# Two attention layers on one core: statistics, weight preparation and one subtraction of the second attention stage moved to other rounds

## The reference

```
x = x + attn_b(layernorm(x))      # q,k,v = x @ W + b; softmax(q k^T / 2) v; @ Wo + bo
x = x + ffn(layernorm(x))         # x @ (weight * scale).T + bias
```

## Time and profile before

| | |
|---|---|
| median of 3 runs | 1218.68 us (1216.99 to 1219.45) |
| profiled execution | 1217.67 us, span 1215.9 us |
| mean granted TensorE clock | 0.848 |
| PE busy | 998.3 us (82%) |
| PE weight loads | 879.1 us (72%) |
| DVE busy | 717.8 us (59%) |
| ACT busy | 367.5 us (30%) |
| POOL busy | 318.7 us (26%) |
| chain that ended last | PE 58%, DVE 22%, issue 6%, POOL 4% |

### The profile page before, as it was taken

The page is one execution under the profiler, slowest core; times in us unless marked ns, Lnnn a source line. Parts: engine busy times, 40 slices in busy tenths (PEclk is TensorE's granted clock), DMA queues, the critical chain, the costliest instruction groups (busy, mean ns, idle before and its releaser), DMA issues.

```text
span 1215.9 us, 21334 instructions
## 1 busy us (share of the span) xinstructions
PE 998.3 (82%) x8146; PEld 879.1 (72%) x8146; DVE 717.8 (59%) x1323; ACT 367.5 (30%) x663; POOL 318.7 (26%) x352
## 2 busy tenths in 40 slices
PE   3589987656378877777888999998888887799998
PEld 3466655446267766655657999998888887799998
DVE  4468876344476678888675545445566655644453
ACT  2136554403122212334334322321122221232232
POOL 4101221024853754212111022100333332230000
PEclk9679999877778888999769999986677775599999
DMA  8736340000020000455420000235666665210000
GB/s 232 218 110 178 115 133 2 2 0 10 26 71 18 1 1 18 141 164 174 130 71 1 2 1 1 62 79 105 131 130 118 144 120 97 35 36 10 18 18 18
DMA packets 147430, 89.38 MB, mean 74 GB/s; under 512 B 109633, under 2 KB 136257, under 8 KB 146561
## 3 DMA queue, kind: packets, MB, share of 16 engines
q1 hardware_dynamic: 142960, 70.45, 24.1%
q10 hardware_dynamic: 2944, 12.59, 3.6%
q0 software_dynamic: 1424, 4.98, 1.4%
HBM read 54.16 MB, written 33.55 MB: 72 GB/s over the span
## 4 chain that ended last, share of the span: by engine, by line
PE 58%; DVE 22%; issue 6%; POOL 4%; ACT 4%; SPq 3%; DMA 2%; DVEq 0%; ACTq 0%; POOLq 0%
PE SC L373 15%; PE SC L2144 9%; PE OT L373 8%; PE pb L373 7%; PE pa L373 5%; DVE mx L1318 3%; PE OT L1892 3%; PE SC L1845 2%; PE OT L2171 2%; PE SC L1874 2%; DVE OS L1486 2%; PE pa L2339 2%; DMA b_Q<-q_groups 1%; PE SC L2050 1%; DVE ON L1675 1%
## 5 line engine op out<-in xcount | busy, mean ns | idle before, releaser
L373 PE MATMUL SC<-xT_h,w_h 128*128 128x256 f32 x512 | 147.3, 288 | 10.3 <-DVE xT_l L1735 7.8
L373 PE MATMUL SC<-xT_l,w_h 128*128 128x256 f32 x512 | 145.8, 285 | 0.0
L373 PE MATMUL SC<-xT_h,w_l 128*128 128x256 f32 x512 | 145.0, 283 | 0.0
L373 PEld LDWEIGHTS SC<-xT_h,w_h 128*128 128x128 f32 x512 | 97.5, 190 | 13.9 <-DVE xT_l L1735 11.5
L373 PE MATMUL OT<-w,Qs 128*128 128x256 f32 x768 | 104.3, 285 | 2.2 <-DVE Qs L1745 1.4
L1318 DVE TENSOR_REDUCE mx<-SC 128x4 f32<-128x1024 f32 x64 | 78.1, 1221 | 43.5 <-PE SC L1845 43.1
L373 PEld LDWEIGHTS OT<-w,Qs 128*128 128x128 f32 x768 | 96.5, 191 | 2.9 <-DVE Qs L1745 1.6
L373 PEld LDWEIGHTS SC<-xT_h,w_l 128*128 128x128 f32 x512 | 97.9, 191 | 0.0
L373 PEld LDWEIGHTS SC<-xT_l,w_h 128*128 128x128 f32 x512 | 97.2, 190 | 0.0
L1741 DVE TENSOR_TENSOR hidden_f<-SC,silu_gate 128x512 f32<-128x512 f32 x64 | 44.1, 689 | 75.5 <-ACT silu_gate L1198 75.5
L2339 PE MATMUL pa<-ident,xn 128*128 128x128 f32 x192 | 35.8, 318 | 62.0 <-DVE xn L1451 27.1
(11 more groups left out here) (413 smaller groups left out, 2684.9 us busy)
## 6 DMA issues: line engine op xcount, KB each, us to landing
Qs<-q_stack SPq DMA_DIRECT2D x56, 128.0 KB, 3.1
k_stack<-KT_h SPq DMA_DIRECT2D x16, 256.0 KB, 2.4
k_stack<-KT_l SPq DMA_DIRECT2D x16, 256.0 KB, 3.0
q_stack<-QT_h SPq DMA_DIRECT2D x16, 256.0 KB, 2.6
q_stack<-QT_l SPq DMA_DIRECT2D x16, 256.0 KB, 3.3
b_Q<-q_groups SPq DMA_DIRECT2D x64, 64.0 KB
o_groups<-b_O ACTq DMA_DIRECT2D x8, 512.0 KB, 3.0
Qs<-q_stack SPq DMA_DIRECT2D x56, 64.0 KB, 3.2
```

The source lines that it names most:

```text
L373: ins = pe.matmul(out_ap, left[a], right[b], start=first and n == 0, stop=last and n == len(terms) - 1, **more)
```

## The change: what it does

Nothing is added or removed; instructions are moved among rounds.

- B0 `stats` goes from offset -17 to -21, `rstd_of` from -16 to -20. `normalise` stays at -14.
- GpSimd's jobs get other rounds. The four r1 weights come at -19, -11, -3 and 5 (before 1, 3, 5, 7), w1 at 13 (10), b1_q at 16 (22), w3 at 21 (16), b1_k 24 (24), b1_v 30 (26), b1_o 32 (28), w2 at 46 (40). The butterflies come at 29, 31, 37, 38, 39 and 45 (before 32 to 37), the mask products from 48 (46).
- VectorE's `x_low` of B0 comes ahead of `heads_out` in its round.
- F3's normalise, bias, transposes and low part come one round later.

```diff
--- before.py
+++ after.py
@@ -426,7 +426,7 @@
             return due(n, 31 + offset if s == F1 else offset)
 
         H_SLOTS = {F1: dict(stats=1, rstd=2, xn=3, bias=4, xT=5, low=6, y=7, res=7),
-                   F3: dict(stats=1, rstd=2, xn=3, bias=4, xT=4, low=5, y=7, res=8)}
+                   F3: dict(stats=1, rstd=2, xn=4, bias=5, xT=5, low=6, y=7, res=8)}
 
         def h_psum(s, b):
 
@@ -731,7 +731,8 @@
                     pool.sem_inc(stack_clear, 1)
 
             A0_JOBS = {8: "f0", 24: "b0_q", 32: "b0_k", 40: "b0_v", 48: "b0_o"}
-            B0_JOBS = {1: "r1_q", 3: "r1_k", 5: "r1_v", 7: "r1_o", 10: "w1", 16: "w3", 22: "b1_q", 24: "b1_k", 26: "b1_v", 28: "b1_o", 40: "w2"}
+            B0_JOBS = {-19: "r1_q", -11: "r1_k", -3: "r1_v", 5: "r1_o", 13: "w1", 16: "b1_q", 21: "w3", 24: "b1_k", 30: "b1_v", 32: "b1_o", 46: "w2"}
+            BUTTERFLIES = (29, 31, 37, 38, 39, 45)
 
             for K in K_rings["attn_a0"]:
                 for r in (32, 96):
@@ -820,16 +821,16 @@
                 if st.kind == "narrow":
                     return narrow_at
                 def wide_at(g):
-                    for b in due(g, -16):
+                    for b in due(g, -20):
                         rstd_of(b)
                     for b in due(g, -13):
                         row_bias(b)
                     if g in B0_JOBS:
                         prepare([B0_JOBS[g]])
-                    if 32 <= g < 38:
-                        butterfly(g - 32)
-                    if 46 <= g < 62:
-                        cut_mask(g - 46)
+                    if g in BUTTERFLIES:
+                        butterfly(BUTTERFLIES.index(g))
+                    if 48 <= g < 64:
+                        cut_mask(g - 48)
 
                 return tokens_at if st.kind == "tokens" else wide_at
 
@@ -1502,11 +1503,11 @@
                             maximum(b, t)
                     for b in due(g, 5):
                         max_low(b)
+                    for b in due(g, -12):
+                        x_low(b)
                     for c in range(CT):
                         for b in due(g, 10 + 2 * c):
                             heads_out(b, c)
-                    for b in due(g, -12):
-                        x_low(b)
                     for b in due(g, 13):
                         a_low(b)
                     for b in due(g, -10):
@@ -1517,7 +1518,7 @@
                         low(b, b0_Q, pb, "qh", bq, "ql")
                     for b in due(g, -5):
                         v_out(b)
-                    for b in due(g, -17):
+                    for b in due(g, -21):
                         stats(b)
                     for b in due(g, -14):
                         normalise(b)
```

## The result

The changed kernel takes 1202.9 us (median of 11 executions, 1200.4 to 1206.2) where the kernel before takes 1218.7 (11 executions): a ratio of 0.9877 with a 95% interval from 0.9848 to 0.9905. The gain is 15.8 us. I had forecast 26.1, and 1202.9 is above the upper end of my range. The profiled execution took 1206.06 us with a span of 1204.3 and a mean granted clock of 0.846. First the page of the changed kernel: busy times, and the granted clock in 40 slices of about 30 us.

A forecast was written before the change was run, and what follows sets the result against it. GpSimd's late root left a hole in B0; chain and residual adds set its beat. 18.9 - 1.4 + 4.4 + 5.35 - 0.3 - 0.9 = 26.1 off 1217.67 gives 1191.6, or 1192.6 as median; range 1181.5 to 1200.5.

The forecast's parts named there:

- steps 1 to 3: B0's fill, its hole at element 3, then its beats element by element; together 26.1 us gained.
- the fill: B0's first rounds up to 312.3 us: nothing changes; 0.3 to 1.0 us if VectorE's cover is gone.
- element 1: B0's beat of element 1: w3's subtraction delays F3's first normalise; 25.4 against 24.0, 1.4 us lost.
- elements 5 to 7: B0's last beats: F3's normalise stands ahead of work that others await; 0.3 and 0.9 us lost.
- Step 2, the hole: Normalise of element 3 runs at once at 312.3; first residual add at 326.6 instead of 345.47, 18.9 us gained.
- after 330: Sign of being wrong: B0's first residual add standing after 330 us, where 326.6 was forecast.
- Step 1: The fill: with GpSimd's jobs spread, roots of elements 1, 2 and 3 come in time; nothing changes up to 312.3.
- Elements 2 to 4: B0's beats: 22.2 for elements 2 and 3 (4.4 us gained), 22.0 for element 4 (5.35 gained).
- B: Rival: F3's normalise and `a_low` mostly miss the long subtractions; 3.3 and 4 to 5 us back, 1184.5; chance 0.17.
- C: Rival: GpSimd's tensor_scalar holds the port too, delaying normalise of elements 0 to 2; up to 4.5 us more, 1197; chance 0.06.
- D: Rival: the order gives nothing, as F3's later transposes limit the beat and low clock stays; about 1199.5; chance 0.10.
- E: Rival: slower, as GpSimd's spread jobs each hold VectorE for their whole length; 1231; chance 0.03.

The follow-up runs named there:

- second pair of profiles: Kernel before and changed kernel profiled again, a comment their only edit; median times 1216.1 and 1199.1 us.
- d_before3: Kernel before with three VectorE memsets (1.5 us of delay) ahead of retention's first mask product; 1228.3 us in one execution.
- p_stats: Kernel before with only B0's statistics and root moved four rounds forward; 1201.0 us, ratio 0.9857.
- p_statsjobs: Kernel before with statistics forward and GpSimd's jobs, butterflies and masks moved, VectorE's order and F3 as before; 1197.9 us, ratio 0.9838.
- u_f3: Changed kernel with F3 back in its old rounds, low part of x still ahead of the divisions; 1194.1 us, ratio 0.9827.
- n_ports: Changed kernel with w1 at round 5, r1_o at 13, w3 at 22 and four of six butterflies one round later; 1185.1 us, ratio 0.9779.
- u_order: Changed kernel with `x_low` back behind the divisions, F3's later rounds kept; 1191.0 us, ratio 0.9808.
- r_after: Changed kernel again, a comment its only edit; 1199.1 us, ratio 0.9869 to the kernel before.
- n_best: Changed kernel with F3's old rounds, w1, r1_o, w3 and butterflies moved, and long copies and subtractions cut in four; 1187.5 us, ratio 0.9728.

## Why the prediction was wrong, point by point

**The step that failed** is the sentence of the sum "Later stages take the shift over whole, since they hang on the same rounds and no transfer there has a time of its own." Rounds and transfers were right, and the clock was left out. The retention stage gave back 7.4 us (6.4 by the second pair of profiles), as busy time of TensorE at the lower granted clock. The size is shown by four profiles of the two kernels. One execution of `d_before3` has such a loss from a delay alone. That the shift of this change did it, and not one of its edits in another way, is likely but not shown.

It isn't the only step that failed. B0 itself gave 21.4 and 17.5 us in the two pairs of profiles where steps 1 to 3 add up to 26.1: the terms for the fill, element 1 and elements 5 to 7 were too favourable, as below. By the medians the change is 10.3 us short of the forecast on the first chip and 9.1 on the second, so on the second B0's shortfall of 8.6 covers it nearly alone. How the medians' shortfall divides between B0 and retention stays open.

**Step 2, the hole: right.** By the profile normalise ran at 316.55 instead of 312.3. Of these 4.2 us, 2.6 are the later start of B0 and 1.6 a longer fill. In it the lower clock was granted for 22.0 us (272.79 to 316.55), against 13.7 before (270.15 to 312.3); my "0.3 to 1.0" for the fill was meant for VectorE's lost cover. That the clock made the 1.6 is not shown. From there to the first residual add I had 14.3 us and it took 14.3 (330.83 - 316.55), with the 4.26 of `a_low` in it. The first add stood "after 330", which I had called a mark of being wrong; without B0's later start it stood at 328.2.

**Step 1: right where it mattered.** The roots were in time. The step did not see that they would have been in time without the jobs moved as well (`p_stats`). Their spreading pays in the beats instead: elements 1 to 3 take 20.3 + 23.2 + 23.15 in `p_statsjobs` against 30.1 + 24.15 + 24.6 in `p_stats`, 12.3 less, and the rest of B0 stays within 0.7.

**Element 1: the term was mis-sized.** I had 25.4, and it took 27.3 and 25.8; with the beat after it, 49.1 and 49.3 against my 47.6. The collision was the forecast one, 4.91 for 0.73. Its price in the beat is 5.9 to 8.1 us (27.3 and 25.8 with it, 19.2 in `u_f3` and 19.9 in `n_ports` without), 1.4 to two times its own 4.2. Both runs differ from the changed kernel in more than this collision, so the price is an estimate from their beats. I had counted the 4 us once, from a base that was too slow. That the rest is the lower clock after the pause is my reading; no run separates it.

**Elements 2 to 4: right, and 1.8 better.** Forecast 22.2, 22.2 and 22.0, measured 21.8, 21.5 and 21.35. In the second profile they took 23.5, 21.5 and 21.7, so there nothing was better.

**Elements 5 to 7: mis-sized.** I had them lose 1.2 and they lost 4.0 (5.5 in the second pair). The two edits don't add up here. The three beats take 56.75 with neither (`p_statsjobs`), 60.1 with the order alone (`u_f3`), 61.8 with F3's later round alone (`u_order`) and 61.9 with both. So F3's later round is enough for all of it, and what lengthens these beats was not followed up.

**The sum again with what was measured:** 26.1 - 2.6 (start of B0) - 1.6 (fill) - 1.9 (element 1) + 1.8 (elements 2 to 4) - 2.8 (elements 5 to 7) - 7.4 (retention) = 11.6, and the two profiled spans differ by 11.6. The start of B0 differs from execution to execution; without it the sum is 14.2, and the medians differ by 15.8.

**The rivals.** B, that the collisions miss, did not happen, but its price was right in kind: `n_ports`, which makes them miss, has a B0 9.7 to 12.9 us shorter than the changed kernel, where B took 7.3 to 8.3 off. That its median of 1185.1 stands beside my 1184.5 is luck, as its chip runs the kernel before in 1213.7; 0.9779 of 1218.7 is 1191.8. C was half right: a GpSimd tensor_scalar does hold VectorE back, for part of its pass (below). The time it gave, 1197, asked for whole passes of 2.0 us in the fill, and the fill shows 0.1 to 0.4 us at each. D, that the order gives nothing, was right by its sum, and I had given it 0.10: over the whole of B0 `x_low` ahead of the divisions gives nothing that can be told, and F3's round takes away 7.1 to 11.3 (204.3 against 211.4 to 215.1 with the order, 201.3 or 204.7 against 212.6 without). Its reason was another, though. The order does give 2.4 at elements 2 and 3, and the beats from 4 on are longer with it. None of the rivals had the clock of a later stage in it, and E had looked for a loss at the wrong place.

## What to carry to other kernels

When an early stage gets faster, compare the busy times of the stages that the edit doesn't touch before judging it: here one execution with a delay of 1.5 us ahead of retention took 8 to 9 us more there, as much as a good edit, and a forecast's range has to hold such a swing. Compare the medians too: the profiled execution of `r_after` was 10 us slower than its median. Test the parts of a bundled edit by themselves: the two lines for the statistics brought as much as the whole change, and F3's later round was a loss in B0. Where a long pass of GpSimd meets a short instruction of VectorE on the path, move the pass or cut it, since by the beats here the pause cost up to about twice its length.

## What the runs showed of the hardware that I had not expected

**GpSimd's tensor_scalar holds VectorE for part of its pass.** Beside 5.40 us of it (399.56 to 404.96) a two-input instruction of 0.69 took 3.72, from 400.05 to 403.77: it ended 1.2 us ahead of the pass. `u_f3` (3.71, until 410.92, the pass until 412.10) and `n_best` show the same. In the fill, beside passes of 1.9 to 2.1 us over 128x512, the pair of normalise took 1.03, 0.82 and 1.16 in the changed kernel and 0.76 in the one before. In `n_best` an `a_low` that lay wholly inside such a pass (323.14 to 323.83, the pass 322.58 to 324.52) took its plain 0.69. Beside a subtraction it is held to the end of the pass: 4.26 from 324.04, so until 328.30, where the subtraction ends at 323.21 + 4.54 = 327.75 and the instruction alone needs 0.69. The Trainium skill (SBUF — State Buffer, "Who interferes with whom") has VectorE and GpSimd share a port pair as an exclusive lock for whole instructions. The subtractions agree with it, the long tensor_scalar only in part, and the short one of `n_best` not at all.

**The lower clock of retention came in a pattern that repeats, that of other stages less so.** The 18 profiles have 34 to 82 us of it in retention, at nearly one idle time of TensorE (28.9 to 33.9), and two executions of `p_statsjobs` on two chips agree to 0.1 us; those of the kernel before differ by 1.1, of the changed one by 0.2. Each microsecond at the lower clock goes with 0.31 us more of the stage. Other stages differ without an edit. B0 took 201.3 and 204.7 us with the same instructions. From retention's last residual to that of the last attention stage (B1) the profiles have 397.8 to 404.2 us, with 167 to 181 us at the lower clock (correlation 0.94); there the two executions of the changed kernel are 3.3 us apart (400.9 and 404.2), those of `p_statsjobs` 2.7. This was not followed up.
